# A new order of steps on five engines in a one-core fp32 audio tower

## What is computed

```python
h = tok(x)                     # 5 frames of context -> 128 features, relu, batch norm over all tokens
h = h + attn0(layernorm(h))    # softmax attention, 8 heads of 16, 0.1 added inside a band of 5
h = h + ffn0(layernorm(h))     # 8 experts, the top 2 count, gelu (erf), hidden size 256
h = h + attn1(layernorm(h))    # linear attention: elu(q)+1, elu(k)+1, causal, value size 64 per head
h = h + ffn1(layernorm(h))     # causal attention, 2 heads of 64, then 8 experts, gelu (tanh), hidden size 512
```

## Time and profile before

| | us |
|---|---|
| runs | 4311.36, 4313.2, 4319.83 |
| median | 4313.2 |
| the profiled execution: its span | 4319.1 |
| token stage | 0 to 169 |
| START | 169 to 402.4 |
| thirty rounds | 402.4 to 4168.4 |
| END | 4168.4 to 4319.1 |

### The profile page before, as it was taken

One profiled execution on the slowest core, in us unless ns is written; L12 is line 12 of the kernel. 1 busy time (PEld: TensorE's weight loads), 2 busy tenths in 40 slices (PEclk: granted clock), 3 DMA queues, 4 the chain that ended last, 5 costly groups with the idle time before them and its releaser, 6 DMA issues.

```text
span 4319.1 us, 104773 instructions
## 1 busy us (share of the span) xinstructions
PE 4066.8 (94%) x41344; PEld 3009.8 (70%) x41344; DVE 3367.6 (78%) x8878; ACT 2784.5 (64%) x4796; POOL 2596.6 (60%) x2494
## 2 busy tenths in 40 slices
PE   7678999999999999999999999999999999999998
PEld 3346777777777777777777777777777777777766
DVE  3357888888888888888888888878888887888876
ACT  3235766666676666667666666766666676666654
POOL 2034666666666666666666666666666666666656
PEclk9779999999999999999999999999999999999999
DMA  4200000011100001110000111000101100010000
...
DMA packets 136939, 127.62 MB, mean 30 GB/s; under 512 B 28928, under 2 KB 135360, under 8 KB 136448
## 3 DMA queue, kind: packets, MB, share of 16 engines
...
## 4 chain that ended last, share of the span: by engine, by line
PE 56%; DVE 24%; ACT 6%; POOL 5%; issue 4%; DMA 3%; SPq 2%; ACTq 0%; DVEq 0%; POOLq 0%
PE pf L1301 9%; PE pf L1303 8%; PE pf L1302 8%; PE pa L1561 8%; DVE h L1285 4%; PE pa L1447 3%; DVE hid_hi L1266 3%; PE pa L1543 3%; PE pa L1346 2%; PE pa L1433 2%; POOL inv_norm L650 2%; PE pa L1301 2%; ACT xn L726 2%; PE pa L1641 2%; PE pa L1303 2%
## 5 line engine op out<-in xcount | busy, mean ns | idle before, releaser
L660 POOL TENSOR_TENSOR hid_lo<-hid,hid_hi 128x504 f16<-128x504 f32 x1536 | 1835.5, 1212 | 775.8 <-DVE hid_hi L1266 775.8
L886 ACT ACTIVATE hid<-pf,vec 128x504 f32<-128x504 f32 x1536 | 1014.7, 680 | 505.5 <-PE pf L1303 356.9
L1301 PE MATMUL pf<-w_hi,hid_hi 128*126 128x128 f16 x6144 | 1133.7, 224 | 10.7 <-DVE h L1285 10.2
L1303 PE MATMUL pf<-w_hi,hid_lo 128*126 128x128 f16 x6144 | 1115.8, 221 | 0.0
L1302 PE MATMUL pf<-w_lo,hid_hi 128*126 128x128 f16 x6144 | 1115.4, 221 | 0.0
L1301 PEld LDWEIGHTS pf<-w_hi,hid_hi 128*126 128x126 f16 x6144 | 844.1, 137 | 153.5 <-issue 53.2
L1302 PEld LDWEIGHTS pf<-w_lo,hid_hi 128*126 128x126 f16 x6144 | 843.8, 137 | 28.5 <-issue 0.2
L1266 DVE CAST hid_hi<-hid 128x504 f16<-128x504 f32 x1536 | 845.4, 573 | 8.2 <-ACT hid L886 2.7
L1303 PEld LDWEIGHTS pf<-w_hi,hid_lo 128*126 128x126 f16 x6144 | 845.2, 138 | 0.0
L1285 DVE SCALAR_TENSOR_TENSOR h<-pf,gates,h 126x128 f32<-126x128 f32 x2048 | 574.1, 342 | 155.2 <-PE pf L1303 152.6
L616 POOL TENSOR_TENSOR pt<-pt,band 126x262 f32<-126x262 f32 x512 | 351.2, 707 | 527.6 <-ACT pt L773 527.4
...
## 6 DMA issues: line engine op xcount, KB each, us to landing
qk_spread<-terms SPq DMA_DIRECT2D x224, 126.0 KB, 2.5
...
```

The source lines that it names most:

```text
L660: nc.gpsimd.tensor_tensor(hid_lo[:, c % 8], hid[:, c % HIDS], hid_hi[:, c % 8], ALU.subtract).then_inc(hid_lo_done[c % 2], 1)
L886: nc.scalar.activation(hid[:, c % HIDS], pf[:, c % 2, 0:TOK], func, bias=vec[:, bias:bias + 1]).then_inc(F["hid_ready"], 1)
L1301: nc.tensor.matmul(out, ah, bh, start=start, stop=False, skip_group_check=skip)
L1303: return nc.tensor.matmul(out, al, bh, start=False, stop=stop, skip_group_check=skip)
```

## The change

The fifteen strings (START, ROUND and END of SP, POOL, ACT, DVE and PE) are replaced. Each new string has the same number of every letter as the old one, so every engine runs the same steps as before, each kind of step still in its own order. Steps of different letters change places. The strings of the token stage, the buffers, the semaphores and the steps themselves stay. For PE's ROUND string the diff reads:

```diff
...
-PE_ROUND = ("lhhoalhhaoaoloahlohloaoohlhhlaooahlahohalolhalahllaaoolahollhholallhhalaaolaoloahhaolahhlhoohaoo"
-          "laahlhhlaohaoohlolqhoohalolaaohaoohhhoqqqlholhalhloqlolhlolollhhlooqlhhqololhhoohhoolll")
+PE_ROUND = ("lhhalohoaohaloahlohololhqhahhoaloalohahholalhoaloalalaohloolholhalallhhalhalaoalhhaooahlahaholho"
+            "aloqoalhohhooalohqhlalaooaoolhahohahllohoholhlolhlqohlololhlhaqlohlqholqoholhoolhlholol")
...
```

More of the change, by code:

```diff
@@ L166 @@
[L166 to L179, removed]
@@ L187 @@
[L187 to L193 removed]
+SP_START = ("qqoqaaaohqqaahhlqaaahaallqaaaqqaqhaaaahoaaahhhaoahaahhoqahlahaoqaaqahaaqlllolaaolloaaloaaaaoaaao"
+            "hallqohoooaahllaalhalqaalaloqalaoaalahholaoohlhlllaaoloahhhhlqalllhhoallllhlhlqoqollllolllohlhlq"
+            "olhloohho")
@@ new lines @@
+SP_ROUND = ("lhlahaooaahooaollooolhaaooloalohlhlalhlllhhalhahohhaolllolaaalaaqlalahhhalaoaollhlohaollhoqhhaha"
+            "ahollhoohohhooloooolqlhhllhlohahahllhoolaqhhhoaohohhhlaolqhhqqhhhooloohallllolooloooloh")
+SP_END = ("hllhhohloholhlohlllloloolhloollhhlllohohhloolhhhhlhhohohloolhllllllllhhoollhohllhllolooohoololoo"
+          "olhlhlhlolhhloohohhhloohohhhllohhooooohhooohohhhhohooooohohhhoooohhooohooohh")
+POOL_START = ("qoqqqqqaqaaaaaaaaaaaaaaaaaaaqaaahahhhaqahqhhahhhqahhhoahhhqallaaqaaaooalllalalalaalaaqlaoaoaoaao"
+              "aooloalaloqaalalllloaaqahllllaoolhlolaoqhlhloalhloaohohhllhlhqhllqlalllholaqlhoqhhhoahohllllolol"
+              "olhoooolh")
@@ new lines @@
+POOL_ROUND = ("loloaalholhhaoaaohaalholhhalhohqlolhlloaallahohaolhaaoohahohlllaahalhhlohoolalaaolhhooaooallhhqh"
+              "loolooholhhaoololhhlaaolholhlahhhhlholoollqqhlllhooqalhqhoaaahhlllololhoqhhoooooalolhho")
+POOL_END = ("llohlolohlohoolholllhllhohlllhohhlhhllhlolhloolooooohlhllllllooolhhholhollololhhlloohhohhhhoohhh"
+            "loolhlhlolhlhlhoooooohhhoolohlhloohooooooolhholhhohoohhhhooohoohhohohooohhhh")
+ACT_START = ("aaqqaaqqaqoqaqaaaaaaaaaaaaaaaaaqaaaahqhaohhhlhaahhhhqahaqhqhoaqhhqhaoallaallalloolaaalaaaoaaalao"
+             "llaloaqoaaaaallaoolaollqlaahhllqoholohllllaaahohhlololooohallhahhlhllholqollohllqlhqolllqhololhh"
+             "ollhhoolo")
@@ new lines @@
+ACT_ROUND = ("aaahhloooahlaloloohhlhhaoohaololoahhaoolhllhhaalllahoalhlholhalllooaqhaahlahaaholoolhoalahhlhaoa"
+             "hqlloaholhqholoooaoohlhaoaloahhaoohohlhllohloolaohllqooolhlhhlqhlhloqoholqhlhlhoolloalh")
+ACT_END = ("hloollloohollhlhohhhllhlhlooolhlhhohlolohololohloollolhlloolhllhhlololohllhoohhlohloooholhollllh"
+           "llhllololhoohohollhlhhohlhooohohohohoohoohoohohhhohhooohohhhoohhooohhohhohoh")
+DVE_START = ("qqqqqqqaaaaaaaaaaaaaaaaaaaaaoaaaaqaaqaqhhhahhaahoohhohqohoohoqhqhoohaoqhoohooaolaalalalllllaalaa"
+             "aaalaaalaoalllaaaaqallqalaalalaaalahllllhhlhlalhhlholoohlhallolhqhllllolqhhlqoollhoqloollhlohlhq"
+             "lhohlohoo")
@@ new lines @@
+DVE_ROUND = ("loahahohalloohallloahooolohahalhohalaalhooalalohaooahlhlhohlaollllahhalolohqhaahaloaohhalalhhhoo"
+             "alolhaolqoohahoohalhoqollahaaolhahhhoollooolloholhqhhololhlalhlhqhlqolohqoolhhollohohll")
+DVE_END = ("ollhlohlllohloholhohllholohhlllhhllhoolhllolhollhloollolhlloohhlolhoohollhoohlolohololhlllohlhlh"
+           "hololhlhhoolllhhhohlooohhhohooohhhooohooohhhohohooohhhhoohhoohhohhhoooohoooo")
+PE_START = ("qqqqqqqaaaaaaaaaaaaaaaaaaaaaaqaaaqaahahhhhhhqhaooaahhhoqqooohlhohaoqohohqoooooaoaaalllalllaaalal"
+            "qalalaaaalaalalaaaqlalalalaaalhlhahlhallalhlhaqlhholloloollhhhohqhqlloallllhohllolqlloloqollhhlo"
+            "hlhlhoooo")
```

16 lines of the change are left out of this document (2 added, 14 removed).

## The result

| kernel | runs | median, us |
|---|---|---|
| before | 4311.36, 4312.33, 4313.2, 4319.83 | 4312.76 |
| changed | 4445.44, 4476.91, 4485.63, 4491.87 | 4481.27 |

The ratio is 1.0374, with a 95% interval of 1.0334 to 1.0414. The forecast was 4321 and the range ended at 4352. The changed kernel is slower, and twenty times as much as the sum said.

The account below looks back on a forecast made before the run. PE was taken as the bound, so that only its waits could change. Thirty rounds at +0.4 us gave +12, START -4, END 0: +8 us, from 4313.2 to 4321 us, with a range of 4282 to 4352.

Parts of the forecast that it names:

- the l chain: PE's waits at the l steps of a round: gives 2.2 us, pays 1.2, so -1.0 a round (+0.15 to -1.75).
- l.4 and l.8: Store of l.4 0.5 us later (0 to 0.65); PE's wait for the transfer at l.8 +1.0 a round (+0.3 to +1.4).
- l.25: ACT's copy of l.24, with a gelu and layer norm put ahead of it: +0.35 us a round (0 to +0.66).
- l.28: PE's wait of 0.69 us ahead of l.28, with more cover ahead of it: -0.4 a round (0 to -0.69).
- The wait ahead of l.29: PE's wait of 0.15 us ahead of l.29 in a round: it also goes.
- l.33, l.37, l.47: PE's waits of 0.61, 0.77 and 0.35 us ahead of these steps: -0.45, -0.75 and -0.25 a round.
- l.29 to l.32: PE's cover falls from 10.96 to 9.75 us, so the wait ahead of l.32 grows by 1.2 a round (1.0 to 1.2).
- Table loads: Five more a round on ACT, four among the exps a.9 to a.16: +0.1 us a round (0 to 1.28).
- START: Stretch ahead of the rounds: linear attention steps start sooner and first up steps fill in, -4 us (-10 to +5).
- END: Stretch after the rounds: l.8 bound by the same transfer, fillers move behind it, 0 us (-5 to +5).
- The sum for the rounds: All terms of one round together: +0.45 us, rounded down to +0.4, thirty rounds +12.
- the second: Rival: gelus and table loads among ACT's exps make PE wait about 1.28 us more a round; 4350 us, chance 0.25.

Follow-up runs that it names:

- e1: The changed kernel with the gates (a.28) ahead of the cast of h0.2 on DVE, as before the change: 4364.4 us, where before is 4323.1.
- e7: The kernel before with gelu h1.16 on ACT moved between the exps of a.11 and a.12, two more table loads a round: 4350.0 us, before 4321.4.
- e5: The kernel before with the START and END strings of the changed kernel, ROUND strings as before: 4344.8 us, where before is 4323.1.
- e11: The changed kernel with the adds of o0.1 moved ahead of the casts of h0.5 and h0.6 on DVE: 4475.2 us, where before is 4326.5.

## Why the prediction was wrong

**The bound.** PE is the bound, and a round changes only by PE's waits: right. What failed is the next sentence. The prediction took the five waits that were there, and one more, as the places where something could change. A wait of zero has no row. It followed the l chain with its cover, step by step, and did not follow a.28 to a.29, which had nothing to show but 0.28 us of margin; nor did it follow the hand-back of the down steps' banks by DVE's adds. The step that failed is this one: the hand-over from a.28 to a.29 was put at nothing, and no reason was given. The runs showed 1.95 us of PE there in every round, and behind it the clock and the second collision; together they are the 3.9 us a round that e1 gives back.

**The length of an operation.** The sum used durations as fixed. The row that could have told otherwise was in it: DVE's scaling L1215, 2.16 us, taken as its length. All its instances, shortest, median and longest in ns, before and changed:

```profile
L1215 DVE TENSOR_TENSOR v<-v,inv_norm x32: 1224/2153/2156, 372.7 to 4245.7; 126x1024 f32<-126x1024 f32 x32
```

```profile
L1215 DVE TENSOR_TENSOR v<-v,inv_norm x32: 1206/1208/1356, 382.5 to 4402.0; 126x1024 f32<-126x1024 f32 x32
```

Its own length is 1.21 us. Before, POOL's L660 had started 0.06 us ahead of it, and held it:

```profile
2505.86 3.22 POOL L660 TENSOR_TENSOR hid_lo<-hid,hid_hi 128x504 f16<-128x504 f32 x2
```

The Trainium skill ("SBUF — State Buffer", section "Who interferes with whom") states the rule: a DVE instruction with two inputs in SBUF contends with a GpSimd instruction that reads SBUF, the port pair that they share is an exclusive lock, and the order of issue decides who blocks. The runs here agree: 0.19 us became 1.92 behind a POOL operation of 1.89, and stayed 0.19 when it came 0.07 ahead. By this rule a cast ahead of the gates was a risk with a price, and the prediction did not weigh it.

**l.4 and l.8.** The store was to come 0.5 later (0 to 0.65), l.8 to wait 1.3 instead of 0.31. In the changed kernel L1543 waits 34.7 us for the transfer, in e1 39.1, 1.2 to 1.3 a round for 0.31: right. The "1.0" of the sum is what was measured, on the mean; the single waits go from 0.59 to 1.92, so not 1 us or more in every round. The store came 0.8 later from the round's start (2519.06 from 2503.50, for 2428.84 from 2414.10). PE now also waits 0.45 at a.3 (L1409, at 2511.39), which the sum had not; whether that makes the store later was not tested. SP of the changed kernel:

```profile
2519.06 0.37 SPq L457 DMA_DIRECT2D terms<-ot_hi  x1
```

The group of L1543 in the changed kernel, with those that answer to the earlier trace rows:

```profile
L1543 PE MATMUL pa<-qk_spread 128*126 128x126 f16 x1536 | 162.8, 229 | 39.0 <-DMA qk_spread<-terms 34.7 <-DVE pt L1177 3.2
L1614 PE MATMUL pa<-pt 64*126 64x126 f32 x256 | 47.4, 322 | 5.9 <-ACT pt L843 0.8 <-DVE pt L1223 0.6
L1603 PE MATMUL pa<-ident,v 126*128 126x126 f32 x256 | 39.2, 305 | 5.1 <-DVE v L1215 5.1
L1630 PE MATMUL pa<-ident,pt 126*126 126x126 f32 x192 | 31.8, 274 | 1.2 <-DVE o L1223 0.7 <-ACT fs L861 0.5
L1367 PE MATMUL pa<-b,gate_t 128*126 128x128 f32 x512 | 77.7, 300 | 0.9 <-ACT gate_t L736 0.4
```

**l.25** (+0.35): no wait there, the term was void. **l.28** (-0.4): its 0.69 is gone altogether (L726 is waited for six times in all, for 34 before). The wait ahead of l.29, taken as 0.15, was 0.36 in the row at 2496.28 of the kernel before, and is gone too. **l.33, l.37, l.47** (-0.45, -0.75, -0.25): the brackets of 0.61, 0.77 and 0.35 are all gone, as the rows show; right, and somewhat small. **l.29 to l.32** (+1.2): 5.1 us in all, none of it in a round, so wrong as it stands. In e1, without a collision at a.29, PE waits 0.40 and 0.95 us for DVE's adds between ACT's copies and l.32, and comes to l.32 just as L1215 ends. So about the time that the term foresaw is spent, in another place and for another reason.

**Table loads** (0.1, with 1.28 as the end): PE's weight loads wait 42.0 us for the exps where they waited 30.9, so 0.4 a round at most. PE's own matmuls wait 2.2 us in all for them in both kernels, so how much of it costs time is not shown. e7 gave 0.9 for two loads at another place. The term is inside its bounds.

**START** (-4, from -10 to +5): +21.9 in the trace, +21.7 in e5. The term was read off the steps that came sooner and not off those that were left without cover at the end of the chain, and it had no part for PE's own matmuls, which took 9.8 us more in e5, at a lower mean clock. **END** (0): +1.6, right.

**The sum for the rounds** was +0.45. Without the collision (e1) a round is 126.13 us for 125.53, +0.60. That the sum is near is luck in good part: +1.2 at l.32 and +0.35 at l.25 did not come, the l chain's waits gave back 0.6 more than forecast, and what came instead stood in no term, +1.7 for DVE's adds at the down steps (61.4 for 10.2 us in all) and +0.4 at a.3 (23.6 for 11.8). And the term that decided was missing. Of the rivals, the second had the sign and the wrong mechanism, and no rival named POOL.

How the 3.9 us a round divide, by the traces of the changed kernel and of e1: 1.95 is the wait at a.29, 0.65 more wait for DVE's adds (80.8 for 61.4 us in all), 1.4 more busy time at the lower clock, and 0.15 less wait at l.8. What is not settled is what each part would be worth alone. In e11 the time at 1.2 GHz was 68 us instead of 100 and the round as long as in the changed kernel, so the parts are not independent. Of the 41 us that e1 keeps, some 22 are START and END (e5), and 18 are the 0.60 a round.
